# A routed feed-forward kernel: the shared part runs beside the routing and ahead of the experts, slots are inverted by scatters to a DRAM table, and expert tiles add their partner's row and scatter to the output

## The reference

```
x2d = hidden.reshape(4096, 512)                       # D = 512, I = 256, E = 8, K = 2
shared = silu(x2d @ shared_gate_w) * (x2d @ shared_up_w) @ shared_down_w
logits = x2d @ router_w                               # [4096, 8]
top_val, top_idx = top_k(logits, 2)
probs = zeros.at[row, top_idx].set(sigmoid(top_val))
xin = probs.T[:, :, None] * x2d[None]                 # each expert's input rows are scaled
gate, up = split(einsum('etd,edf->etf', xin, gate_up_w), 2)
expert_out = einsum('eti,eid->etd', silu(gate) * up, down_w)
return x + (shared + expert_out.sum(axis=0)).reshape(...)
```

## Time and profile before

| | us |
|---|---|
| median of three runs | 1340.28 |
| the profiled execution's own time | 1340.52 |
| its span, first to last instruction | 1338.6 |
| attention, to 674.1 | 674.1 |
| routing, 674.1 to 738.2 | 64.1 |
| experts, 738.2 to 1171.1 | 432.9 |
| shared part and sum, 1171.1 to the end | 167.5 |

### The profile page before, as it was taken

The page is one execution under the profiler, slowest core; times in us unless marked ns, Lnnn a source line. Parts: engine busy times, 40 slices in busy tenths (PEclk is TensorE's granted clock), DMA queues, the critical chain, the costliest instruction groups (busy, mean ns, idle before and its releaser), DMA issues. The chain is left out here.

```text
span 1338.6 us, 21991 instructions
## 1 busy us (share of the span) xinstructions
PE 1228.1 (92%) x5564; PEld 687.0 (51%) x5565; DVE 684.0 (51%) x1178; ACT 530.6 (40%) x992; POOL 694.7 (52%) x602
## 2 busy tenths in 40 slices
PE   5899999999999999999814799999999999899998
PEld 2445544545455444544314344444444444489997
DVE  4676676667767666777179112221222122136666
ACT  1465566656656665656410222222222222221211
POOL 1487787778778777878638222222222222034543
PEclk7799999999999999999855799999999999989999
DMA  6645644554555456442081332233222222158886
GB/s 177 180 132 151 160 134 125 153 159 126 143 159 144 118 157 159 123 116 73 16 327 66 98 99 84 89 94 94 85 88 94 93 88 85 71 171 271 282 275 226
DMA packets 93921, 183.54 MB, mean 137 GB/s; under 512 B 11664, under 2 KB 14224, under 8 KB 93888
## 3 DMA queue, kind: packets, MB, share of 16 engines
q1 hardware_dynamic: 81856, 145.38, 36.3%
q0 software_dynamic: 10880, 35.66, 8.5%
q10 hardware_dynamic: 1152, 2.10, 0.6%
HBM read 129.02 MB, written 51.97 MB: 135 GB/s over the span
## 5 line engine op out<-in xcount | busy, mean ns | idle before, releaser
L710 DVE TENSOR_REDUCE row_max<-bank 128x1 f32<-128x512 f32 x512 | 343.5, 684 | 179.8 <-PE bank L536 179.1
L649 ACT ACTIVATE probsT<-bank 128x512 f32<-128x512 f32 x512 | 300.1, 596 | 233.2 <-PE bank L548 231.0
L408 POOL TENSOR_TENSOR key_sum<-key_sum,probsT 128x1024 f32<-128x1024 f32 x128 | 299.5, 2368 | 0.4 <-ACT probsT L649 0.4
L536 PE MATMUL bank<-k_stack,q_stack 96*128 96x512 f32 x512 | 283.3, 557 | 13.2 <-DMA q_stack<-q_hi 6.4
L1238 PE MATMUL bank<-gate_up_sb,rows_T 128*128 x576 | 273.1, 597 | 1.6 <-ACT rows_T L1173 1.6
L404 POOL TENSOR_TENSOR key_sum<-probsT 128x1024 f32<-128x1024 f32 x64 | 151.3, 2377 | 131.3 <-ACT probsT L649 131.3
L548 PE MATMUL bank<-q_stack,k_stack 99*128 99x512 f32 x512 | 207.2, 406 | 1.3 <-ACT probsT L649 1.1
L536 PEld LDWEIGHTS bank<-k_stack,q_stack 96*128 96x128 f32 x512 | 98.9, 194 | 170.7 <-DVE row_max L710 126.2
L1238 PEld LDWEIGHTS bank<-gate_up_sb,rows_T 128*128 128x128 f32 x576 | 104.6, 192 | 106.4 <-issue 106.4
L1124 POOL COPY row_prob<-slot_prob 128x1 f32 (+1 forms) x72 | 13.1, 182 | 258.4 <-DVE rows_scaled L1139 255.3
L558 PE MATMUL bank<-probsT,vals 128*32 128x512 f32 x1024 | 136.5, 605 | 0.1
(11 more groups left out here) (141 smaller groups left out, 1531.6 us busy)
## 6 DMA issues: line engine op xcount, KB each, us to landing
expert_rows_dram<-rows_out SPq DMA_DIRECT2D x72, 256.0 KB, 2.1
k_stack<-hi_dram SPq DMA_DIRECT2D x60, 256.0 KB, 4.1
q_stack<-hi_dram SPq DMA_DIRECT2D x60, 256.0 KB, 6.5
x_row<-in_x SPq DMA_DIRECT2D x16, 512.0 KB, 3.6
hidden_dram<-hid SPq DMA_DIRECT2D x16, 512.0 KB, 4.9
gate_up_sb<-in_L_ffn_gate_up_w SPq DMA_DIRECT2D x8, 1024.0 KB, 12.6
tok<-hidden_dram SPq DMA_DIRECT2D x16, 512.0 KB
x_in<-in_x SPq DMA_DIRECT2D x16, 512.0 KB
```

Of the source, the lines that this page charges most:

```text
L408: nc.gpsimd.tensor_tensor(total, total, probs(k), ALU.add).then_inc(added, 1)
L536: nc.tensor.matmul(logit_bank[i % 2][:, :], q_stack[par][g][0:K_LOGIT, h, q * P:(q + 1) * P], k_stack[par][g][0:K_LOGIT, h, :], start=True ...
L649: nc.scalar.activation(probsT[:, j, :], key_bank[j % 2][:, :], ACT.Exp, scale=SCALE).then_inc(probs_ready, 1)
L710: nc.vector.tensor_reduce(row_max[g][:, i:i + 1], logit_bank[i % 2][:, :], AX.X, ALU.max)\
```

## The change

- The shared weights are loaded in the last attention batch into buffers that attention no longer uses, and split there: ACT makes the high parts between exponentials, POOL the low parts after its last sum.
- SP writes zeros over the whole of `expert_rows_dram` (18.9 MB in 16 DMAs, one in each attention batch).
- The hidden rows go to `rows_ext`, a table `[4096, 2, 512]`: half 0 of a row is the hidden row, half 1 is later filled with shared part plus `x`.
- Routing and the shared part are one block. PE runs the shared part's 16 batches; DVE's routing chain is cut in pieces and written between its steps of the first six batches. The expert weights are loaded one expert after every second batch.
- Inversion: for each slot a record of four 32-bit numbers (token, probability, partner slot, output row). DVE makes the records by token; POOL scatters them in 64 indirect DMAs of 128 records of 16 bytes to `slot_table_dram`, and SP loads the table back at the end of the block.
- Experts: POOL gathers 4 KB rows (hidden and shared-plus-x) into a ring of four buffers. DVE, no longer ACT, takes `down`'s result out of PSUM, twice: `add_rest` adds the row's half 1 and SP stores that sum to `expert_rows_dram`, and `add_partner` adds the row that the token's other expert stored, which POOL gathers from that table. Of a token's two slots the later one has a partner slot and an output row; the earlier one has a number that is out of range in both fields, and such rows are skipped. POOL scatters the final rows to the output. The fourth block is gone.

`NT` stays 72. The diff, cut:

```diff
@@ sync of attention
+            def clear_rows(b):
+                n = NT * P // B
...
+                sp.dma_start(dst, zero_rows[0:n // r, :].unsqueeze(1).broadcast_to([n // r, r, T]))\
+                    .then_inc(rows_cleared, 16)
...
             def body(b, kind, par):
                 for g in range(G):
...
+                    if g == 0 and kind == LAST:
+                        sp.wait_ge(qm_ready, UNITS)
+                        for dst, src in zip(shared_raw, (sh_gate_w, sh_up_w, sh_down_w)):
+                            sp.dma_start(dst, src.rearrange("(k p) i -> p k i", p=P)).then_inc(shared_loaded, 16)
...
                     if exists(kind, g, 3):
                         store_split(*place(b, par, g, 3), 1)
+                    if g == 0:
+                        clear_rows(b)
@@ gpsimd and scalar of attention
             rows(pool, body)
+            for n, (hi, lo, raw) in enumerate(zip(shared_hi, shared_lo, shared_raw)):
+                pool.wait_ge(shared_hi_ready, n + 1)
+                nc.gpsimd.tensor_tensor(lo[:, :, :], raw, hi[:, :, :].bitcast(F32), ALU.subtract)
...
                     exp(b, g, j)
                     empty_misc(b, kind, par, s)
+                    if kind == LAST and g == 1 and j in (4, 8, 12):
+                        act.wait_ge(shared_loaded, 48)
+                        hi, raw = shared_hi[j // 4 - 1], shared_raw[j // 4 - 1]
+                        nc.scalar.activation(hi[:, :, :], raw, ACT.Copy).then_inc(shared_hi_ready, 1)
@@ the block of routing and shared part
+            @block2.sync
...
+                store(B - 1)
+                sp.wait_ge(scattered, 16 * 2 * TT)
+                sp.dma_start(slot_info[:, :, :], slot_table.rearrange("(p n) c -> p n c", p=P)).then_inc(info_loaded, 16)
...
+                pool.wait_ge(info_ready, 1)
+                for c in range(2):
+                    for t in range(TT):
+                        nc.gpsimd.indirect_dma_start(slot_table[:, :],
+                                                     bass.IndirectOffsetOnAxis(ap=table_row[:, c, t:t + 1], axis=0),
+                                                     info[:, c, t, :], None).then_inc(scattered, 16)
@@ gpsimd of the experts
-                    nc.gpsimd.tensor_copy(row_prob[i][:, :], slot_prob[:, bass.ds(n, 1)])
-                    nc.gpsimd.tensor_copy(row_no[i][:, :], slot_token[:, bass.ds(n, 1)]).then_inc(row_no_ready, 1)
...
+                def gather(n, i):
+                    if not first(n, DEPTH):
+                        pool.wait_ge(out_ready, n - DEPTH + 1)
+                        passed()
+                    nc.gpsimd.tensor_copy(row_info[i][:, :], slot_info[:, bass.ds(n, 1), ROW:PROB + 1].rearrange("p o c -> p (o c)"))\
+                        .then_inc(row_info_ready, 1)
+                    pool.wait_ge(row_info_ready, n + 1)
+                    passed()
+                    nc.gpsimd.indirect_dma_start(rows_in[i][:, :, :].rearrange("p a t -> p (a t)"), None,
+                                                 rows_ext.rearrange("r a t -> r (a t)"),
+                                                 bass.IndirectOffsetOnAxis(ap=row_info[i][:, ROW:ROW + 1], axis=0))\
+                        .then_inc(gathered[i], 16)
+                def gather_partners(n, i):
+                    if not first(n, 1):
+                        pool.wait_ge(stored[(i - 1) % 2], turns(n - 1, i - 1, 2) + 16)
+                        passed()
+                    if not first(n):
+                        pool.wait_ge(final_ready, n - 1)
+                        passed()
+                        pool.wait_ge(final_scattered[i % 2], turns(n, i, 2))
+                        passed()
+                    nc.gpsimd.tensor_copy(link_info[i % 2][:, :],
+                                          slot_info[:, bass.ds(n, 1), PARTNER:].rearrange("p o c -> p (o c)"))\
+                        .then_inc(link_info_ready, 1)
+                    pool.wait_ge(link_info_ready, n + 1)
+                    passed()
+                    nc.gpsimd.indirect_dma_start(partner_rows[i % 2][:, :], None, expert_rows[:, :],
+                                                 bass.IndirectOffsetOnAxis(ap=link_info[i % 2][:, 0:1], axis=0),
+                                                 bounds_check=NT * P - 1, oob_is_err=False)\
+                        .then_inc(partner_gathered[i % 2], 16)
+                def scatter(n, i):
+                    pool.wait_ge(final_ready, n + 1)
+                    passed()
+                    nc.gpsimd.indirect_dma_start(out_rows, bass.IndirectOffsetOnAxis(ap=link_info[i % 2][:, 1:2], axis=0),
+                                                 rows_final[i % 2][:, :], None,
+                                                 bounds_check=TOKENS - 1, oob_is_err=False)\
+                        .then_inc(final_scattered[i % 2], 16)
+                def step(n, i):
+                    if exists(n + 2):
+                        gather(n + 2, (i + 2) % DEPTH)
+                    if exists(n - 2):
+                        scatter(n - 2, (i - 2) % DEPTH)
+                    if exists(n - 1):
+                        gather_partners(n - 1, (i - 1) % DEPTH)
@@ vector and tensor of the experts
+                def add_rest(n, i):
+                    dve.wait_ge(down_done, n + 1)
+                    if not first(n):
+                        dve.wait_ge(stored[i % 2], turns(n, i, 2))
+                    nc.vector.tensor_tensor(rows_out[i % 2][:, :], out_bank[i % 2][:, :], rows_in[i][:, 1, :], ALU.add)\
+                        .then_inc(out_ready, 1)
+                def add_partner(n, i):
+                    dve.wait_ge(partner_gathered[i % 2], turns(n, i, 2) + 16)
+                    if not first(n):
+                        dve.wait_ge(final_scattered[i % 2], turns(n, i, 2))
+                    nc.vector.tensor_tensor(rows_final[i % 2][:, :], out_bank[i % 2][:, :], partner_rows[i % 2][:, :], ALU.add)\
+                        .then_inc(final_ready, 1)
                 def step(n, i):
+                    if exists(n - 2):
+                        add_rest(n - 2, (i - 2) % DEPTH)
...
                 def down(n, i, e):
...
-                        pe.wait_ge(out_copied, n - 1)
+                        pe.wait_ge(final_ready, n - 1)
```

More of the change, by code:

```diff
@@ new lines, in upper_sh @@
+                def upper_sh(b):
+                    act.wait_ge(sh_done, b + 1)
+                    if b >= 2:
+                        act.wait_ge(shared_done, 2 * (b - 1))
+                    nc.scalar.activation(sh_hi[b % 2][:, :, :], sh[:, :, :], ACT.Copy).then_inc(sh_hi_ready, 1)
+                copy_tokens(0)
+                for b in range(B):
+                    if b == 1:
+                        act.wait_ge(best_ready, 1)
+                        nc.scalar.activation(sigm[:, :, :], best[:, :, :], ACT.Exp, scale=-1.0).then_inc(sigm_ready, 1)
+                    if b + 1 < B:
+                        copy_tokens(b + 1)
+                    silu(b)
+                    upper_sh(b)
@@ L970, in link, with choose @@
                     dve.wait_ge(chain, done[0])
[L972 to L976 removed]
+                def choose(c, src):
                     link(v.tensor_reduce(best[:, c, :], src[:, :, :], AX.X, ALU.max))
@@ new lines, in _ @@
+                dve.wait_ge(constants_ready, 3)
+                choose(0, logits_all)
+                choose_second()
+                for b in range(B):
+                    if b + 1 < B:
+                        lower_tokens(b + 1)
+                    combine(b)
+                    lower_sh(b)
+                    if b == 0:
+                        copy_counts()
+                    if b >= 1:
+                        add_x(b - 1)
+                    if b == 1:
+                        add_up_tiles()
+                    if b == 2:
+                        lay_out_tiles()
+                    if b == 3:
+                        find_slots()
+                    if b == 4:
+                        describe_slots()
+                    if b == 5:
+                        name_experts()
@@ L1109, in first @@
-            def first(n):
-                return isinstance(n, int) and n < 2
+                for n in range(DEPTH):
+                    step(n, n)
+                with eng.Fori(1, NT // DEPTH - 1) as n:
+                    for i in range(DEPTH):
+                        step(DEPTH * n + i, i)
+                for n in range(NT - DEPTH, NT + 3):
+                    step(n, n % DEPTH)
+            def first(n, m=2):
+                return isinstance(n, int) and n < m
             def exists(n):
@@ L1115, in exists, with turns, passed @@
                 return not isinstance(n, int) or 0 <= n < NT
+            def turns(n, i, ring, each=16):
+                return n // ring * each if isinstance(n, int) else each // ring * (n - i % ring)
+            out_rows = out.rearrange("b d t -> (b d) t")
             @block3.gpsimd
             def _(pool):
```

(26 more changed lines are left out.)

771 lines of the change are left out of this document (339 added, 432 removed).

## The result

| | us |
|---|---|
| before, median of four runs | 1339.01 (1337.64 to 1340.99) |
| changed, median of four runs | 1418.64 (1418.21 to 1421.15) |
| ratio, 95% interval | 1.0597 (1.0577 to 1.0618) |
| profiled execution of the changed kernel, span | 1416.8 |

The change makes the kernel 6.0% slower. The direction was forecast; the time was not: 1364 was said, with a range that ended at 1412. Busy time by stretch, columns as in the earlier trace rows: attention, then from SP's first token load to the first row gather (routing and shared part), then experts.

A forecast was written before the change was run, and what follows sets the result against it. PE was taken as the bound except in routing, where DVE is busy. From 1340.5: -64.1 routing, +1.0 attention, +6.7 shared stretch, +1.8 start, +71.3 for tile waits, the rest a longer end: 1364, range 1310 to 1412.

The forecast's parts named there:

- The step that failed: Routing and shared part in one block: PE's 16 batches cost 167.5 as before; 174.2 with the other terms.
- rival C: Experts: the loops bind harder, Loop B 7.3, Loop A up to 7.9; at 7.5, 1415; chance 0.10.
- an expert block that starts after 860: Sign at the start of the experts, expected near 849: would prove the cover of the table scatters wrong.
- The period: Experts: 6.8 us per tile (6.7 early, 7.0 late), 489.6 for 72, with PE waiting about 1.0 in each.
- Loop A: Experts, ring of four row buffers: sum, next row gather, landing and scaling closed in a loop, 6.71 us per tile.
- Loop B: Experts: partner gather waits behind scatter, partner sum and previous partner gather; 6.43 us per tile, 6.85 for the last experts.
- The rest: End of the experts after 72 periods: last turn and down, sums, store, partner gather and scatter, 14.9 us.
- Attention: End of attention: ACT's first copy of a shared weight adds 1.0 us (0 to 1.2); POOL's low parts add nothing.
- Rival E: Attention: the zeros delay logits by 1 us in each batch, 1380; chance 0.04.
- I count no fall: Experts: PE's clock does not fall although PE waits about 1.0 us in each tile.
- rival D: POOL's table scatters outlast the shared part; at 2.0 us each +21 or more, 1386; chance 0.06.
- The width of the gather: Experts, row gather of 512 KB: the 256 KB more add 0.84 us to a landing of 3.64.

The follow-up runs named there:

- experiment 2: Changed kernel with each token load issued one step earlier on SP, same bytes and expert loads: 1376.34 us, ratio to before 1.0283.
- experiment 5: As experiment 2, with POOL's partner gather ahead of the scatter and the ring still at four buffers: 1355.36 us, ratio to before 1.0124.
- experiment 4: Changed kernel with a ring of eight row buffers instead of four: 1414.75 us, ratio to before 1.0577.
- experiment 9: As experiment 8, with POOL's copies one step ahead of the DMAs that read them: 1285.78 us, ratio to before 0.9624.
- experiment 11: As experiment 9, with a second clear in each attention batch into a table that nothing reads: 1333.28 us, ratio to before 0.996.
- experiment 10: As experiment 5, with the row gather half as wide (256 KB in place of 512), only its time read: 1306.87 us.
- experiment 6: Changed kernel with token loads one step earlier, ring of eight buffers and partner gather ahead of the scatter: 1330.59 us, ratio to before 0.9944.
- experiment 8: As experiment 6, with POOL gathering rows three tiles ahead instead of two: 1292.36 us, ratio to before 0.9661.

## Why the prediction was right and where it failed

The sum, term by term. gate_up(0) is the first `gate_up` matmul of the experts; a period is the mean distance of row gathers.

| | predicted | changed | with experiment 2 |
|---|---|---|---|
| block starts | 675.1 | 670.2 | 671.1 |
| gate_up(0) starts | 858.4 | 895.2 | 852.1 |
| 72 periods | 489.6 (6.80) | 500.6 (6.95) | 502.8 (6.98) |
| rest, to the end | 14.9 | 21.0 | 20.0 |
| span | 1362.9 | 1416.8 | 1374.9 |

**The step that failed** is "What is late next is PE. Its 16 batches cost what they did, 167.5 with their ends". From the block's start to gate_up(0) the prediction had 183.3; it took 225.0, which is 41.7 of the 53.9 that are missing. With experiment 2 it took 181.0, so the other terms of that sum (first load, counts, store, table) hold within 3 as a sum. The prediction counted the token loads only once, the first one, at 4.1. The section on the change lists the expert loads as moved between the batches; the prediction did not ask what stands behind them in SP's queue, nor that PE now turns the tokens 5.6 earlier than before. Both were in the order of the two kernels, and the prices were in the rows: 3.34 us per MB for the 2.5 MB ahead gives 8.4. No rival held it either; rival C's 1415 came near the time for another reason. Against experiment 2 the way to gate_up(0) is 44.0 longer: the waits for tokens are 31.8 more (36.6 against 4.8), and PE's 1092 matmuls of the stretch take 12.9 more at the lower clock (168.27 against 155.38). The sign "an expert block that starts after 860" came true (the first row gather starts at 888.4), but it was to prove that the table scatters were not covered, and those were over at 823: the sign pointed at the wrong cause.

**The period** was right in mechanism and 0.15 short, 11 us in the sum; its shape was right too, 6.83 early and 7.14 late against 6.7 and 7.0. The waits before `rows_scaled` are longer than the 2 us that were said, 222.0 in 70 or 3.2 each. Loop A came out at 6.62 by its rows against 6.71 (landing 4.29 against 3.64 + 0.84). Loop B was mis-sized, 7.19 in the round shown against 6.43 to 6.85: POOL's wake before the scatter is 0.92, not 0.57, and the landing 3.49, not 3.22. Loop A without B gives 6.78 (experiment 5), and with the ring opened B gives 6.99 (experiment 4); in the changed kernel A is the larger in the first half and B in the second, where most slots have a partner. The forecast's direction was not luck: with the token loads mended (experiment 2) the kernel is still 2.8% slower, by the loops and the end behind them, and both had to be opened, and the third behind them, before the routing's gain was seen. The third loop, over the store, stood in no sum of the prediction.

**The rest** of 21.0 against 14.9: the last sum of `add_rest` starts 7.3 behind the 72 periods (895.2 + 500.6 to 1403.08), where 2.3 was taken for turn and down, and that is 5.0. The last scatter starts 3.6 after its sum, where 0.92 is usual, another 2.7; why is open, and in experiment 9 it is 0.9. The links between came out 1.6 shorter.

**Attention** ended 4.9 before the forecast, 1.0 of which was for ACT's copies. Why the other 3.9 are gone was not tested; in the first 100 us PE had already done 302 matmuls at clock 0.86, against 287 at 0.83 in the kernel before. POOL's low parts lay beside PE's last work as said. No cost of the zeros shows where they stand: the loads of `k_stack` from `hi_dram` land in 6.3 at the median instead of 4.1, but PE's waits for stacks do not grow (6.5 in all, against 8.7 before). Rival E was wrong for this kernel; the kernel without zeros was not tried. Experiment 11 shows that the cover has no room for the same again in the other unit.

**The clock.** "I count no fall" held in the experts (0.97). The fall behind the six waits is part of the step that failed. The rows had a fall behind a pause of 3.3; experiment 11 has falls behind waits of 2.4.

**The table scatters**, rival D, were hidden as said:

```profile
L1026 POOL DMA_INDIRECT slot_table_dram<-info,table_row x64: 963/967/1481, 741.3 to 822.4; - x64
```

(822.4 - 741.3) / 63 = 1.29 each against 1.25, done long before the last store at 878.8, and in experiment 2 still 17 before it. A cost of their 16 bytes, which the Trainium skill's rule on writes under 512 bytes (DMA: Bandwidth & Descriptors, "Specifications") would put in the DMA engines, could not be seen from POOL's side.

The width of the gather: 4.4 against 3.8 is 0.6 for 256 KB, and 0.84 was taken. The Trainium skill's rule in "Anatomy of one DMA — SWDGE (gpsimd) path" of the same page gives 0.60, which this pair bears out; experiment 10 against 5 has 1.0, with the half as wide gathers landing below 3.8.

## What to carry to other kernels

When a large load is moved into a loop, write down for each load behind it in the same queue when it is issued, how many bytes stand ahead of it, and when its reader asks. Here a load with 2.5 MB ahead landed in 10.1 and PE stood 4.5 to 5.8 for it; sent one step earlier, with the same bytes ahead, it cost nothing. Count a wait of the bounding engine with what its clock loses behind it: here 12.9 on top of 31.8, in experiment 11 26.4 on top of 28.2. A software pipeline whose buffers, waits and in-order queue close a loop over a DMA runs at that loop's length, whatever its nominal lead: list every loop with its links and how many tiles it spans, and expect that opening one only shows the next (6.98, 6.78, 6.40, 5.8 in experiments 2, 5, 6 and 8). A busy share is no measure of room: the DMA engines were busy 0.75 with PE never waiting (experiment 2), and 0.71 with PE waiting in every second unit (experiment 11).

## What the runs showed of the hardware

- An indirect DMA on POOL starts 0.30 after the instruction before it when nothing is waited for, 0.81 to 0.90 after a copy on POOL that it waits for, and 0.92 after a DVE result it waits for (the scatters of the changed kernel and of experiment 4).
- After each of six pauses of 4.5 to 5.8 us PE ran at half clock for a while: the next 8 turns took 1.97 in place of 1.03. In experiment 11 waits of 2.4 were enough in some places (granted clock 0.50 behind them), and waits of 1.8 to 2.4 changed nothing in others.
- A direct load of 512 KB with 2.5 MB ahead in its queue landed 10.1 after its issue; with little ahead 4.1 (670.2 to 674.3).
- Partner gathers, of whose rows on average half are skipped, land in 3.1 at the median and 2.1 at least: 2.7 in the first half of the experts, where fewer rows have a partner, and 3.6 in the second. The gathers of 512 KB beside them, all rows present, land in 4.4.
